# Exponentials over 1536 columns with two rings of three banks, in place of 1024 columns with three rings of two

## The chip, the cores and the metric

The kernel runs on one core of a Trainium2 chip. The metric is the device time of one execution in microseconds (us), a median over several runs; lower is better.

## What is computed

One transformer layer over 2048 tokens of 256 features: attention with 16 heads of 16 features, a residual and a layer norm, a gated feed-forward part with int8 weights, a residual and a layer norm. The change touches the attention alone, which is, cut to what matters:

```python
q, k, v = (X @ Wq + bq, X @ Wk + bk, X @ Wv + bv)      # (1, 2048, 256), split into 16 heads of 16
scores = einsum('bhqd,bhkd->bhqk', q, k) / sqrt(16)    # 16 heads x 2048 x 2048
attn = softmax(scores, axis=-1)
out = einsum('bhqk,bhkd->bhqd', attn, v)
x = layernorm(x + out @ Wo + bo)
```

## The kernel before

The program has three stages on one core: the projections to q, k and v (to about 48 us), the attention (about 53 to 564 us) and the output projection with the feed-forward part (to the end). Only the attention is touched.

**Units.** For each of the 16 heads the 2048 keys are cut into 16 tiles of 128 (`TT` = 16). One head with one key tile is called a unit here; there are 256. In a unit, TensorE makes the scores of 128 keys against all 2048 queries: four matmuls of 512 columns (`CH` = 4, `CW` = 512), each filling one bank of PSUM (line 1087). ScalarE takes exponentials of them, PSUM to SBUF, into `probs` (line 510). TensorE then multiplies the exponentials with v and a column of ones (`prob_times_v`, line 1061): four float32 matmuls, which the trace shows as two passes each, eight in all, and which add up in bank `ACC` = 6. This product runs two units behind the scores. So the order of TensorE, written out by hand, is: the four scores of unit u, then the product of unit u-2, then the four scores of unit u+1, and so on. There is no scheduler; each engine runs its own program in order and waits on semaphores.

**The banks before.** Banks 0 to 5 hold scores, as three rings of two. One exponential reads two banks (1024 columns), so a unit has two, its halves. Before the first score of a half, TensorE waits until the exponential three back has left those two banks; the semaphore `exp_done` counts exponentials:

```python
ring = (2 * n + half) % 3
pe.wait_ge(exp_done, 2 * u + half - 2)     # ahead of each pair of scores
pe.wait_ge(exp_done, 2 * (u - 1))          # ahead of the product of unit u-2
```

**The other side.** ScalarE waits with `scores_ready` for the two scores of its half, and ahead of the first half of a unit also with `pv_done` for the product of unit u-3, since `probs` holds three units. Heads 1 to 15 run in a hardware loop of five trips with three heads each; head 0 stands ahead of it.

**At a head's end** VectorE copies the finished accumulator out of bank 6 (line 730, `attn<-ps`), and TensorE waits for this copy (`attn_saved`) before the first product of the next head, which stands behind the scores of that head's third unit. SyncE refills the q and k of a head's slot once `scores_ready` has reached the end of the head that used it (`refill`).

Of the kernel before, what the change touches and what calls it, by code (L numbers as in the profile page):

```python
# [6 lines left out]
def layer_program(nc, X, Wq, bq, Wk, bk, Wv, bv, Wo, bo, w_gate, w_up, w_down, s_gate, s_up, s_down, out):  # L23
# [3 lines left out]
    ACT = mybir.ActivationFunctionType  # L27
# [3 lines left out]
    P = 128  # L31
    S, HID = X.shape[1], X.shape[2]
    NH = 16
# [3 lines left out]
    TT = S // P  # L37
    CW = 512
    CH = S // CW
# [8 lines left out]
    ROWS = MROW + 3  # L48
    LAG = 3
    VW = 32  # L50
    NSLOT = 3
    SCALE = float(HD) ** -0.5
    SAFE = 40.0
# [2 lines left out]
    with ExitStack() as ctx:  # L56
# [3 lines left out]
        def place(name, shape, dt, at=None):  # L60

            size = int(np.prod(shape[1:])) * {f32: 4, f32r: 4, i32: 4, bf16: 2, i8: 1}[dt]
            where = place_at[0] if at is None else at
            if at is None:
                place_at[0] += (size + 63) // 64 * 64
            return nc.alloc_sbuf_tensor_at(name, shape, dt, offset=where)
# [40 lines left out]
        minus_half = place("minus_half", [P, TPC], f32)  # L107
        q_stack = [place(f"q_stack{i}", [ROWS, S], bf16) for i in range(NSLOT)]
        k_stack = [place(f"k_stack{i}", [ROWS, S], bf16) for i in range(NSLOT)]
        v_slot = [place(f"v_slot{i}", [P, TT, VW], f32) for i in range(NSLOT)]  # L110

# [29 lines left out]
        probs = place("probs", [P, 3, CH, CW], f32, at)  # L141
# [2 lines left out]

        ps = ctx.enter_context(nc.psum_tensor("ps", [P, 8, CW], f32))
        ACC = 6

        def sem(name):
            return ctx.enter_context(nc.semaphore(name))
# [43 lines left out]
        bound_zero = sem("bound_zero")  # L193
        stack_loaded = [sem(f"stack_loaded{i}") for i in range(NSLOT)]
        v_slot_ready = sem("v_slot_ready")
        scores_ready = sem("scores_ready")
        exp_done = sem("exp_done")
        pv_done = sem("pv_done")
        attn_saved = sem("attn_saved")
# [50 lines left out]
        V_BANK = [4, 5, 4, 5, 4, 5, 4, 2]  # L250
# [3 lines left out]
        def _(sp):  # L254
# [9 lines left out]
            half = TPC // 2  # L264
# [36 lines left out]
            def load_stack(h, slot, done):  # L301

                for product in range(len(PRODUCTS)):
                    load_q(h, slot, product, done)
                    load_k(h, slot, product, done)
# [6 lines left out]

            def refill(h, slot):

                sp.wait_ge(scores_ready, (h - NSLOT + 1) * 2 * TT)
                load_stack(h, slot, stack_loaded[slot])
                load_shift(h, slot, stack_loaded[slot])


            sp.wait_ge(shift_zero, 2)  # L320
            for s in range(NSLOT):

# [37 lines left out]
            for h in range(NSLOT, NH):  # L360
                refill(h, h % NSLOT)
# [80 lines left out]
                nc.gpsimd.tensor_tensor(rstd[:, 2 * b:2 * b + 2], var_eps[:, 2 * b:2 * b + 2],  # L442
                                        minus_half[:, 0:2], ALU.pow).then_inc(ln2_rstd, 1)

        def three_heads(engine, head):

            head(0, 0)
            with engine.Fori(0, (NH - 1) // 3) as i:
                for j in range(1, 4):
                    head(i * 3 + j, j)  # L450

        @block.scalar
        def _(act):
            act.dma_start(w_raw[:, 0, :].rearrange("p (k n) -> p k n", k=KO),
# [26 lines left out]
            for n, (c, k) in enumerate(QK):  # L481
                parts, b_c = (q_parts, bq_c) if k < 2 else (k_parts, bk_c)
                if n == 0:
# [3 lines left out]
                                     bias=b_c[:, k % 2:k % 2 + 1]).then_inc(part1_ready, 1)  # L487
                nc.scalar.activation(squares[:, k, c * CW:(c + 1) * CW], ps[:, n % QK_BANKS, :], ACT.Square,
                                     bias=b_c[:, k % 2:k % 2 + 1]).then_inc(squares_ready, 1)
# [7 lines left out]
                                       ps[:, V_BANK[p], :].rearrange("p (a b) -> p a b", a=2)).then_inc(v_ready, 1)  # L497


            def head(h, j):  # L500
                for kt in range(TT):
                    u = h * TT + kt
                    for half in range(2):
                        ring = (2 * (j * TT + kt) + half) % 3

                        act.wait_ge(scores_ready, 2 * u + half + 1)
                        if half == 0 and not (j == 0 and kt < 3):

                            act.wait_ge(pv_done, u - 2)
                        nc.scalar.activation(  # L510
                            probs[:, (j * TT + kt) % 3, 2 * half:2 * half + 2, :].rearrange("p a b -> p (a b)"),
                            ps[:, 2 * ring:2 * ring + 2, :].rearrange("p a b -> p (a b)"),
                            ACT.Exp, bias=0.0, scale=SCALE).then_inc(exp_done, 1)


            act.wait_ge(xt_ready, 2 * CH)
            three_heads(act, head)

            act.wait_ge(warm_ready, 2)
            nc.scalar.activation(warm[:], minus_half[:], ACT.Silu)  # L520
# [48 lines left out]
            for b in range(2):  # L569
                i = 2 * b  # L570
                act.wait_ge(tail_mean, b + 1)
                nc.scalar.activation(out_tmp[:, i, :], r_tmp[:, i, :], ACT.Identity, scale=rstd[:, i:i + 1],
                                     bias=neg_mean[:, i:i + 1]).then_inc(tail_scaled, 1)

        @block.vector
        def _(dve):
# [350 lines left out]
        def _(pe):  # L927
# [57 lines left out]
            for n, (c, k) in enumerate(QK):  # L985
# [8 lines left out]
                if n >= QK_BANKS:  # L994
# [3 lines left out]
                i, m = k // 2, k % 2  # L998
# [3 lines left out]
                         first=(n == 0)).then_inc(proj_psum, 1)  # L1002
# [30 lines left out]
            with pe.If(need_exact > 0):  # L1033

                with pe.Fori(0, NH) as h:
                    pe.wait_ge(gen_loaded, (h + 1) * STACK)
                    for t in range(TT):
# [6 lines left out]
                        for b in range(CH):  # L1044
                            last = nc.tensor.matmul(ps[:, 4 * (t % 2) + b, :], q_stack[0][0:SROW, t * P:(t + 1) * P],
                                                    k_stack[0][0:SROW, b * CW:(b + 1) * CW], start=True, stop=True)
# [11 lines left out]
            def prob_times_v(slot, n, kt):  # L1058

                for q in range(CH):  # L1060
                    last = nc.tensor.matmul(ps[32 * q:32 * q + VW, ACC, :], v_slot[slot][:, kt, :],  # L1061
                                            probs[:, n % 3, q, :], start=(kt == 0), stop=(kt == TT - 1))
                last.then_inc(pv_done, 1)

            def head(h, j, i):
                slot, first = j % 3, (j == 0)
                for kt in range(TT):
                    u = h * TT + kt
                    n = j * TT + kt
                    if kt == 0:  # L1070

                        pe.wait_ge(stack_loaded[slot], (i + 1 + j // 3) * (STACK + SHIFT))

                        pe.wait_ge(bound_ready, 1 if first else 2 + slot)
                    if first and kt == 2:
                        pe.wait_ge(bound_ready, 2)
                    for half in range(2):
                        ring = (2 * n + half) % 3
                        if first and kt == 0 and half == 1:

                            pe.wait_ge(rest_ready, len(QK))
                            pe.wait_ge(v_ready, TT // 2)

                        if not (first and 2 * kt + half < 3):
                            pe.wait_ge(exp_done, 2 * u + half - 2)
                        for q in (2 * half, 2 * half + 1):
                            last = nc.tensor.matmul(ps[:, 2 * ring + q % 2, :],  # L1087
                                                    k_stack[slot][0:ROWS, kt * P:(kt + 1) * P],
                                                    q_stack[slot][0:ROWS, q * CW:(q + 1) * CW], start=True, stop=True)
                        last.then_inc(scores_ready, 1)  # L1090

                    if kt >= 2:
                        if kt == 2:
                            pe.wait_ge(v_slot_ready, h + 1)
                            if not first:

                                pe.wait_ge(attn_saved, h)
                        pe.wait_ge(exp_done, 2 * (u - 1))
                        prob_times_v(slot, n - 2, kt - 2)
                    elif not first:  # L1100
                        pe.wait_ge(exp_done, 2 * (u - 1))
                        prob_times_v((j - 1) % 3, n - 2, TT - 2 + kt)


            pe.wait_ge(ones_ready, NSLOT - 1)
            pe.wait_ge(ones_pool, 1)
            pe.wait_ge(ones_loaded, 16 * NSLOT)
            head(0, 0, 0)
            with pe.Fori(0, (NH - 1) // 3) as i:
                for j in range(1, 4):  # L1110
                    head(i * 3 + j, j, i)
            for kt in (TT - 2, TT - 1):
                pe.wait_ge(exp_done, 2 * ((NH - 1) * TT + kt + 1))
                prob_times_v(0, 3 * TT + kt, kt)


# [1 line left out]
            for g in range(8):  # L1118
# [4 lines left out]
                for k in range(8):  # L1123
                    last = nc.tensor.transpose(
                        ps[:, 2 * ug + k // 4, (k % 4) * P:(k % 4 + 1) * P],
                        attn[:, 8 * ug + k, HPB * ko:HPB * (ko + 1), :].rearrange("p r h -> p (r h)"), ident[:])
# [22 lines left out]
            for c, half, ko in steps:  # L1149
# [86 lines left out]
```

## Time and profile before

| | |
|---|---|
| median of 3 runs | 695.58 us (695.06 to 698.11) |
| span of the profiled execution | 694.9 us |
| TensorE matmul busy | 668.3 us, 96% |
| ScalarE busy | 580.7 us, 84% |
| VectorE busy | 153.7 us, 22% |
| exponentials, line 510 | 512 of 1024 columns, 495.2 us busy |
| scores, line 1087 | 1024 matmuls, 267.6 us busy |
| product with v, line 1061 | 2048 matmul passes, 272.5 us busy |

The profile gives one execution by its span, from the first to the last instruction. What lies around the span isn't in it; the median of the runs is 0.7 us above the span. Busy times of TensorE are unions of modelled, overlapping records.

### The profile page before, as it was taken

Reading aid. Unit: us, or ns where it says so; the run is one execution under the profiler, and the core shown is the slowest. Engines: PE = TensorE matmul, PEld = TensorE weight load, DVE = VectorE, ACT = ScalarE, POOL = GpSimd, SP = SyncE. Lnnn points to the kernel's source line nnn. Section 1 sums busy time; section 2 is a strip of 40 time slices with the busy share of each in tenths; the row PEclk is TensorE's granted clock in tenths of the full one; section 3 lists DMA queues with packets and bytes.
Section 4 is the critical chain, followed back from the end, with each engine's and each line's share of the span. In section 5 each row is a group of like instructions: output and inputs, shape, how many; then the busy total and the mean of one; then the engine's idle time right before and its main releaser. Section 6 shows DMA issues by size and latency. Waiting matters only on the chain.

```text
span 694.9 us, 10890 instructions
## 1 busy us (share of the span) xinstructions
PE 668.3 (96%) x4002; PEld 259.4 (37%) x4002; DVE 153.7 (22%) x305; ACT 580.7 (84%) x657; POOL 38.1 (5%) x47
## 2 busy tenths in 40 slices
PE   8979999999999999999999999999999999999994
PEld 7852222222222222222222222222222257788884
DVE  6772000000000000000000000000000047756766
ACT  5748999999999999999999999999999943744442
POOL 3215000000000000000000000003000001000002
PEclk9998999999999999999999999999999999999998
DMA  8066132140404041321404040413000000000001
GB/s 233 19 71 69 13 35 31 17 46 3 46 0 46 0 46 12 34 29 17 45 1 46 0 46 0 46 12 34 0 0 0 0 0 1 1 0 32 0 30 60
DMA packets 15428, 19.50 MB, mean 28 GB/s; under 512 B 5912, under 2 KB 12336, under 8 KB 15408
## 3 DMA queue, kind: packets, MB, share of 16 engines
q1 hardware_dynamic: 14592, 18.97, 20.2%
q10 hardware_dynamic: 816, 0.26, 0.1%
q8 instruction: 12, 0.20, 0.1%
q14 instruction: 8, 0.07, 0.0%
HBM read 4.34 MB, written 2.10 MB: 9 GB/s over the span
## 4 chain that ended last, share of the span: by engine, by line
PE 89%; DVE 5%; issue 4%; ACT 1%; POOL 1%; DMA 1%; POOLq 0%; SPq 0%; DVEq 0%
PE ps L1061 37%; PE ps L1087 36%; PE ps L1184 7%; PE ps L1167 4%; PE ps L966 4%; DMA x_tok<-in_L_attn_X 1%; DVE at L769 1%; DVE stats L785 1%; DVE h L870 1%; PE ps L950 1%; DVE r_tmp L831 1%; ACT sg L549 0%; POOL rstd L431 0%; DVE x_tok L778 0%; PE ps L1155 0%
## 5 line engine op out<-in xcount | busy, mean ns | idle before, releaser
L510 ACT ACTIVATE probs<-ps 128x1024 f32<-128x1024 f32 x512 | 495.2, 1021 | 19.8 <-PE ps L1087 12.5
L1061 PE MATMUL ps<-probs,v_slot 128*32 128x512 f32 x2048 | 272.5, 605 | 4.7 <-issue 4.7
L1087 PE MATMUL ps<-q_stack,k_stack 100*128 100x512 bf16 x1024 | 267.6, 385 | 5.6 <-DVE k_stack L675 5.6
L1087 PEld LDWEIGHTS ps<-q_stack,k_stack 100*128 100x128 bf16 x1024 | 79.7, 98 | 280.8 <-ACT probs L510 213.1
L730 DVE TENSOR_SCALAR attn<-ps 128x512 f32 (+1 forms) x16 | 16.4, 1028 | 488.5 <-PE ps L1061 488.5
L1061 PEld LDWEIGHTS ps<-probs,v_slot 128*32 128x32 f32 x2048 | 40.9, 108 | 114.6 <-ACT probs L510 94.7
L549 ACT ACTIVATE sg<-ps,sgate_c 128x512 f32<-128x512 f32 x32 | 22.1, 690 | 46.7 <-PE ps L1184 46.5
L1167 PE MATMUL ps<-wd,h_hi 128*128 128x256 f32 x128 | 32.2, 285 | 2.3 <-DVE r_tmp L831 2.1
L1167 PE MATMUL ps<-wd,h_lo 128*128 128x256 f32 x128 | 31.9, 283 | 0.0
L870 DVE SCALAR_TENSOR_TENSOR h<-ps,sup_c,sg 128x512 f32<-128x512 f32 x32 | 24.0, 750 | 27.0 <-ACT sg L549 26.2
L1167 PEld LDWEIGHTS ps<-wd,h_hi 128*128 128x128 f32 x128 | 24.3, 190 | 4.9 <-DVE r_tmp L831 3.4
L526 ACT ACTIVATE x_tok<-x_tok,neg_mean,rstd 128x256 f32<-128x256 f32 x16 | 8.3, 591 | 21.3 <-DVE neg_mean L799 21.3
L1184 PE MATMUL ps<-yt_hi,wg 128*128 (+1 forms) x64 | 25.5, 399 | 0.5 <-DVE h L870 0.3
L1184 PE MATMUL ps<-yt_lo,wg 128*128 (+1 forms) x64 | 25.3, 396 | 0.0
L1184 PE MATMUL ps<-yt_hi,wu 128*128 (+1 forms) x64 | 25.0, 391 | 0.0
L1184 PE MATMUL ps<-yt_lo,wu 128*128 (+1 forms) x64 | 24.9, 389 | 0.0
L1167 PEld LDWEIGHTS ps<-wd,h_lo 128*128 128x128 f32 x128 | 24.4, 191 | 0.9
L423 POOL CAST wg<-gate 128x2048 fp32r<-128x2048 int8 x1 | 1.9, 1891 | 409.3 <-DMA q_stack<-shift 409.3
L878 DVE TENSOR_TENSOR h_lo<-h,h_hi 128x512 fp32r<-128x512 f32 x32 | 21.8, 682 | 0.4
L558 ACT CAST h_hi<-h 128x512 fp32r<-128x512 f32 x32 | 19.6, 614 | 1.2 <-DVE h L870 1.2
L1155 PE MATMUL ps<-wo,at 128*128 128x256 f32 x64 | 14.6, 383 | 0.9 <-DVE at L769 0.8
L1184 PEld LDWEIGHTS ps<-yt_hi,wg 128*128 128x128 f32 x64 | 12.1, 190 | 2.5 <-DVE h L870 1.1
(100 smaller groups left out, 354.4 us busy)
## 6 DMA issues: line engine op xcount, KB each, us to landing
q_stack<-q_parts SPq DMA_DIRECT2D x16, 192.0 KB
k_stack<-k_parts SPq DMA_DIRECT2D x16, 192.0 KB
q_stack<-q_parts SPq DMA_DIRECT2D x16, 128.0 KB
k_stack<-k_parts SPq DMA_DIRECT2D x16, 128.0 KB
x_tok<-in_L_attn_X SPq DMA_DIRECT2D x3, 512.0 KB, 8.5
out<-out_tmp SPq DMA_DIRECT2D x3, 512.0 KB, 2.9
k_stack<-k_parts SPq DMA_DIRECT2D x16, 64.0 KB
q_stack<-q_parts SPq DMA_DIRECT2D x16, 64.0 KB
```

The costliest lines, as they stand in the source:

```text
L510: nc.scalar.activation(probs[:, (j * TT + kt) % 3, 2 * half:2 * half + 2, :].rearrange("p a b -> p (a b)"), ps[:, 2 * ring:2 * ring + 2, : ...
L549: nc.scalar.activation(sg[:, m % 2, :], ps[:, m % 2, :], ACT.Silu, scale=sgate_c[:, m:m + 1]).then_inc(silu_done, 1)
L558: nc.scalar.copy(h_hi[:, m - 1, :], h32[:, (m - 1) % 2, :]).then_inc(h_hi_ready, 1)
L730: nc.vector.tensor_scalar(attn[:, :, :, bass.ds(h, 1)], ps[:, ACC, :].rearrange("p (u r o) -> p u r o", r=NH, o=1), 1.0, None, ALU.mult).t ...
L870: nc.vector.scalar_tensor_tensor(h32[:, m % 2, :], ps[:, 2 + m % 2, :], sup_c[:, m:m + 1], sg[:, m % 2, :], ALU.mult, ALU.mult).then_inc(g ...
L878: nc.vector.tensor_tensor(h_lo[:, m - 1, :], h32[:, (m - 1) % 2, :], h_hi[:, m - 1, :].bitcast(f32), ALU.subtract).then_inc(h_ready, 1)
L966: last = nc.tensor.matmul(dst, w(ko), x(ko), start=(n == 0), stop=(n == len(terms) - 1))
L1061: last = nc.tensor.matmul(ps[32 * q:32 * q + VW, ACC, :], v_slot[slot][:, kt, :], probs[:, n % 3, q, :], start=(kt == 0), stop=(kt == TT - 1))
L1087: last = nc.tensor.matmul(ps[:, 2 * ring + q % 2, :], k_stack[slot][0:ROWS, kt * P:(kt + 1) * P], q_stack[slot][0:ROWS, q * CW:(q + 1) * C ...
L1155: last = nc.tensor.matmul(ps[:, b, half * HID:(half + 1) * HID], at32[:, ko, 2 * b + half, :, :].rearrange("p j u -> p (j u)"), wo[:, ko, ...
L1167: last = nc.tensor.matmul(ps[:, 4 + i, 0:HID], h[:, m, i * P:(i + 1) * P], wd[:, m, :], start=(m == 0 and j == 0), stop=(m == MT - 1 and j ...
L1184: last = nc.tensor.matmul(ps[:, bank, :], w[:, ko, m * P:(m + 1) * P], y[:, ko, bass.ds(c * CW, CW)], start=(ko == 0 and j == 0), stop=(ko ...
```

## The change

One exponential now reads three banks (`GROUP` = 3, 1536 columns), and banks 0 to 5 are two rings of three. Scores are counted bank by bank through the whole attention, b = 4n + q; bank b belongs to group b // 3, and group g uses the ring g % 2. Groups no longer end where units end: twelve banks are three units and four groups. There are 341 exponentials of three banks and a last one of one bank. `probs` is used as one ring of twelve banks. Every score matmul now signals `scores_ready`, where every second one did. TensorE waits ahead of each group's first score until the group two back is done. The order of the matmuls is unchanged: four scores, then the product of two units back.

```diff
+    GROUP = 3
+    UNIT = CH
...
+        probs_flat = probs[:].rearrange("p a b n -> p (a b) n")
+        def group_of(bank):
+            return bank // GROUP
...
-                sp.wait_ge(scores_ready, (h - NSLOT + 1) * 2 * TT)
+                sp.wait_ge(scores_ready, (h - NSLOT + 1) * TT * UNIT)
...
+            def exp_group(g, trips, banks, held):
+                first, ring = GROUP * g, 3 * UNIT
+                act.wait_ge(scores_ready, trips * GROUP + first + banks)
+                if held:
+                    act.wait_ge(pv_done, trips * GROUP // UNIT + (first + banks - 1 - ring) // UNIT + 1)
+                nc.scalar.activation(
+                    probs_flat[:, first % ring:first % ring + banks, :].rearrange("p a b -> p (a b)"),
+                    ps[:, GROUP * (g % 2):GROUP * (g % 2) + banks, :].rearrange("p a b -> p (a b)"),
+                    ACT.Exp, bias=0.0, scale=SCALE).then_inc(exp_done, 1)
...
+            for g in range(HEAD0):
+                exp_group(g, 0, GROUP, g >= 4)
+            with act.Fori(0, (NH - 1) // 3) as i:
+                for g in range(HEAD0, HEAD0 + TRIP):
+                    exp_group(g, i * TRIP, GROUP, True)
+            exp_group(HEAD0 + TRIP, ((NH - 1) // 3 - 1) * TRIP, 1, True)
...
-                        if not (first and 2 * kt + half < 3):
-                            pe.wait_ge(exp_done, 2 * u + half - 2)
-                        for q in (2 * half, 2 * half + 1):
-                            last = nc.tensor.matmul(ps[:, 2 * ring + q % 2, :],
+                    for q in range(UNIT):
+                        b = n * UNIT + q
+                        g = group_of(b)
+                        if b % GROUP == 0 and b >= 2 * GROUP:
+                            pe.wait_ge(exp_done, trips + g - 1)
+                        last = nc.tensor.matmul(ps[:, GROUP * (g % 2) + b % GROUP, :],
...
-                        pe.wait_ge(exp_done, 2 * (u - 1))
+                        pe.wait_ge(exp_done, trips + group_of((n - 2) * UNIT + UNIT - 1) + 1)
```

TensorE, head 0, three units. `ps<-q_stack,k_stack` is a score, `ps<-probs,v_slot` the product. Before:

```order
218 L1087 MATMUL ps<-q_stack_82,k_stack_85 128x512 [waits exp_done]
219 L1087 MATMUL ps<-q_stack_82,k_stack_85 128x512
220 L1087 MATMUL ps<-q_stack_82,k_stack_85 128x512 [waits exp_done]
221 L1087 MATMUL ps<-q_stack_82,k_stack_85 128x512
222 L1061 MATMUL ps<-probs,v_slot_88 32x512 [waits exp_done]
223 L1061 MATMUL ps<-probs,v_slot_88 32x512 x3
```

Every unit is the same there: two pairs of scores with a wait ahead of each, then the product. TensorE, the same place, now:

```order
226 L1076 MATMUL ps<-q_stack_82,k_stack_85 128x512 [waits exp_done]
227 L1076 MATMUL ps<-q_stack_82,k_stack_85 128x512 x2
228 L1076 MATMUL ps<-q_stack_82,k_stack_85 128x512 [waits exp_done]
229 L1049 MATMUL ps<-probs,v_slot_88 32x512 [waits exp_done]
230 L1049 MATMUL ps<-probs,v_slot_88 32x512 x3
231 L1076 MATMUL ps<-q_stack_82,k_stack_85 128x512 x2
232 L1076 MATMUL ps<-q_stack_82,k_stack_85 128x512 [waits exp_done]
233 L1076 MATMUL ps<-q_stack_82,k_stack_85 128x512
234 L1049 MATMUL ps<-probs,v_slot_88 32x512 [waits exp_done]
235 L1049 MATMUL ps<-probs,v_slot_88 32x512 x3
236 L1076 MATMUL ps<-q_stack_82,k_stack_85 128x512
237 L1076 MATMUL ps<-q_stack_82,k_stack_85 128x512 [waits exp_done]
```

The wait stands ahead of every third score, so its place moves through the units: in the first of three units ahead of the first and the fourth score, in the second ahead of the third, in the third ahead of the second. A product now lies inside two of every four groups.

ScalarE, the start of head 0, before:

```order
L510 ACTIVATE probs<-ps 128x1024 [waits scores_ready,xt_ready]
L510 ACTIVATE probs<-ps 128x1024 [waits scores_ready] x5
L510 ACTIVATE probs<-ps 128x1024 [waits pv_done,scores_ready]
L510 ACTIVATE probs<-ps 128x1024 [waits scores_ready]
```

and now:

```order
L491 ACTIVATE probs<-ps 128x1536 [waits scores_ready,xt_ready]
L491 ACTIVATE probs<-ps 128x1536 [waits scores_ready] x3
L491 ACTIVATE probs<-ps 128x1536 [waits pv_done,scores_ready] x17
```

Four exponentials cover what six did, and each of them behind the fourth waits for `pv_done` too.

## Rows read from the trace of the kernel before

**Rows 1.** The page, its parts on busy time and on granted clock.
```profile
PE 668.3 (96%) x4002; PEld 259.4 (37%) x4002; DVE 153.7 (22%) x305; ACT 580.7 (84%) x657; POOL 38.1 (5%) x47
...
PEclk9998999999999999999999999999999999999998
```

**Rows 2.** The page, costliest groups: busy us, mean ns of one, idle before.
```profile
L510 ACT ACTIVATE probs<-ps 128x1024 f32<-128x1024 f32 x512 | 495.2, 1021 | 19.8 <-PE ps L1087 12.5
L1061 PE MATMUL ps<-probs,v_slot 128*32 128x512 f32 x2048 | 272.5, 605 | 4.7 <-issue 4.7
L1087 PE MATMUL ps<-q_stack,k_stack 100*128 100x512 bf16 x1024 | 267.6, 385 | 5.6 <-DVE k_stack L675 5.6
```

**Rows 3.** Timeline inside the attention: start us, length us, instructions merged.
```profile
299.69 1.04 PE L1087 MATMUL ps<-q_stack,k_stack 100*128 100x512 bf16 x4
...
300.65 1.06 PE L1061 MATMUL ps<-probs,v_slot 128*32 128x512 f32 x8
...
301.65 1.04 PE L1087 MATMUL ps<-q_stack,k_stack 100*128 100x512 bf16 x4
...
309.52 1.04 PE L1087 MATMUL ps<-q_stack,k_stack 100*128 100x512 bf16 x4
```

**Rows 4.** Timelines of ScalarE and TensorE in short windows of that stretch.
```profile
299.29 2.07 ACT L510 ACTIVATE probs<-ps 128x1024 f32<-128x1024 f32 x2
...
300.33 1.94 ACT L510 ACTIVATE probs<-ps 128x1024 f32<-128x1024 f32 x2
...
299.69 0.60 PE L1087 MATMUL ps<-q_stack,k_stack 100*128 100x512 bf16 x2
```

**Rows 5.** ScalarE groups by form, of the whole program.
```profile
L496 ACT COPY v_all<-ps 128x512 f32<-128x512 f32 x8 | 4.7, 588 | 5.5 <-PE ps L966 5.5
...
L462 ACT ACTIVATE warm<-minus_half 128x4 f32<-128x4 f32 x1 | 0.2, 205 | 0.0
```

**Rows 6.** Timeline at the end of the attention.
```profile
561.78 1.02 ACT L510 ACTIVATE probs<-ps 128x1024 f32<-128x1024 f32 x1
...
562.85 0.13 PEld L1061 LDWEIGHTS ps<-probs,v_slot 128*32 128x32 f32 x4 [0.65 <-ACT probs L510]
...
562.49 1.04 PE L1061 MATMUL ps<-probs,v_slot 128*32 128x512 f32 x8
```

**Rows 7.** Timeline where one head ends and the next begins.
```profile
310.48 1.07 PE L1061 MATMUL ps<-probs,v_slot 128*32 128x512 f32 x8
...
311.48 1.04 PE L1087 MATMUL ps<-q_stack,k_stack 100*128 100x512 bf16 x4
311.74 1.03 DVE L730 TENSOR_SCALAR attn<-ps 128x512 f32 x1 [30.59 <-PE ps L1061]
...
312.87 1.07 PE L1061 MATMUL ps<-probs,v_slot 128*32 128x512 f32 x8 [0.35 <-issue]
```

**Rows 8.** Timeline at the start of the attention.
```profile
52.76 5.28 PE L1087 MATMUL ps<-q_stack,k_stack 100*128 100x512 bf16 x12 [5.55 <-DVE k_stack L675]
...
53.86 5.61 ACT L510 ACTIVATE probs<-ps 128x1024 f32<-128x1024 f32 x6 [6.03 <-PE ps L1087]
```

**Rows 9.** Stretches: length, busy us by engine, granted clock, DMA share, GB/s.
```profile
300.00:400.00 100.00, 98.99 (x604) 23.53 (x602) 3.84 (x6) 97.24 (x102) 0.00 (x0) 1.00 0.23 24
...
44.00:52.00 8.00, 3.20 (x28) 2.94 (x24) 4.23 (x11) 1.39 (x3) 0.37 (x1) 0.97 0.97 108
52.00:58.00 6.00, 5.25 (x16) 1.52 (x18) 4.62 (x9) 4.14 (x5) 0.90 (x1) 0.50 0.84 98
566.00:582.00 16.00, 15.09 (x95) 12.85 (x94) 12.60 (x28) 0.00 (x0) 0.30 (x1) 1.00 0.01 2
```

More of the change, by code:

```diff
@@ L443, in _ @@
                                         minus_half[:, 0:2], ALU.pow).then_inc(ln2_rstd, 1)
[L445 to L450, printed above, removed]
         @block.scalar
@@ L497, in _ @@
                                        ps[:, V_BANK[p], :].rearrange("p (a b) -> p a b", a=2)).then_inc(v_ready, 1)
[L500 to L513, printed above, removed]
-            act.wait_ge(xt_ready, 2 * CH)
-            three_heads(act, head)
+            def exp_group(g, trips, banks, held):
[7 more added lines that the diff above has]
+                    ACT.Exp, bias=0.0, scale=SCALE).then_inc(exp_done, 1)
+            HEAD0 = TT * UNIT // GROUP
+            TRIP = 3 * TT * UNIT // GROUP
+            act.wait_ge(xt_ready, 2 * CH)
+            for g in range(HEAD0):
[4 more added lines that the diff above has]
+            exp_group(HEAD0 + TRIP, ((NH - 1) // 3 - 1) * TRIP, 1, True)
             act.wait_ge(warm_ready, 2)
@@ L1063, in prob_times_v, with head @@
                 last.then_inc(pv_done, 1)
-            def head(h, j, i):
+            def head(j, i):
                 slot, first = j % 3, (j == 0)
+                trips = i * 3 * TT * UNIT // GROUP
                 for kt in range(TT):
-                    u = h * TT + kt
                     n = j * TT + kt
@@ L1076, in head @@
                         pe.wait_ge(bound_ready, 2)
-                    for half in range(2):
-                        ring = (2 * n + half) % 3
-                        if first and kt == 0 and half == 1:
+                    for q in range(UNIT):
+                        b = n * UNIT + q
+                        g = group_of(b)
+                        if first and b == V_BANK[-1]:
                             pe.wait_ge(rest_ready, len(QK))
                             pe.wait_ge(v_ready, TT // 2)
-                        if not (first and 2 * kt + half < 3):
-                            pe.wait_ge(exp_done, 2 * u + half - 2)
-                        for q in (2 * half, 2 * half + 1):
-                            last = nc.tensor.matmul(ps[:, 2 * ring + q % 2, :],
-                                                    k_stack[slot][0:ROWS, kt * P:(kt + 1) * P],
-                                                    q_stack[slot][0:ROWS, q * CW:(q + 1) * CW], start=True, stop=True)
+                        if b % GROUP == 0 and b >= 2 * GROUP:
+                            pe.wait_ge(exp_done, trips + g - 1)
+                        last = nc.tensor.matmul(ps[:, GROUP * (g % 2) + b % GROUP, :],
+                                                k_stack[slot][0:ROWS, kt * P:(kt + 1) * P],
+                                                q_stack[slot][0:ROWS, q * CW:(q + 1) * CW], start=True, stop=True)
                         last.then_inc(scores_ready, 1)
@@ L1093, in head @@
                         if kt == 2:
-                            pe.wait_ge(v_slot_ready, h + 1)
+                            pe.wait_ge(v_slot_ready, i * 3 + j + 1)
                             if not first:
-                                pe.wait_ge(attn_saved, h)
-                        pe.wait_ge(exp_done, 2 * (u - 1))
+                                pe.wait_ge(attn_saved, i * 3 + j)
+                        pe.wait_ge(exp_done, trips + group_of((n - 2) * UNIT + UNIT - 1) + 1)
                         prob_times_v(slot, n - 2, kt - 2)
                     elif not first:
-                        pe.wait_ge(exp_done, 2 * (u - 1))
+                        pe.wait_ge(exp_done, trips + group_of((n - 2) * UNIT + UNIT - 1) + 1)
                         prob_times_v((j - 1) % 3, n - 2, TT - 2 + kt)
@@ L1107, in _ @@
             pe.wait_ge(ones_loaded, 16 * NSLOT)
-            head(0, 0, 0)
+            head(0, 0)
             with pe.Fori(0, (NH - 1) // 3) as i:
                 for j in range(1, 4):
-                    head(i * 3 + j, j, i)
+                    head(j, i)
             for kt in (TT - 2, TT - 1):
-                pe.wait_ge(exp_done, 2 * ((NH - 1) * TT + kt + 1))
+                pe.wait_ge(exp_done, group_of(((NH - 1) * TT + kt + 1) * UNIT - 1) + 1)
                 prob_times_v(0, 3 * TT + kt, kt)
```

## The prediction

> **What bounds the kernel now.** I read the page first. TensorE is busy 96% of the span and ScalarE 84%, and the granted clock is at its upper level, 2.4 GHz, nearly throughout [rows 1]. Three lines carry the attention: the exponentials with 495 us on ScalarE, the scores and the products with 268 and 273 us on TensorE [rows 2]. In a stretch of 100 us both engines look full, 99.0 and 97.2 us busy [rows 9]. So busy time doesn't say which of the two sets the pace, and the timeline must.
>
> In the timeline the units follow each other evenly: scores at 299.69, product at 300.65, scores at 301.65, and five units from 299.69 to 309.52, so 1.966 us a unit [rows 3]. Does TensorE wait for an exponential there? Exponentials start at 299.29, 300.33 and 301.25 (299.29 + 2.07 - 1.02, and 300.33 + 1.94 - 1.02); their distances are 1.04 and 0.92 us in turn [rows 4]. The first two scores of the unit at 299.69 end at 300.29 and the next exponential starts at 300.33, 0.04 us behind them [rows 4]: ScalarE waits for TensorE once a unit. Call that exponential 2u. The scores at 299.69 need only exponential 2u-3, which began some 2 us earlier, at about 297.3, and ended at about 298.3. The second pair needs 2u-2, which began at 298.37 and ended at 299.39; that pair begins at 299.69 + 2 x 0.22 = 300.13, with 0.74 us to spare. (0.22 is the distance of two scores: 0.60 less the 0.38 that one lasts.) **TensorE waits for nothing and sets the pace; ScalarE has about 0.12 us of slack in a unit.** At a head's end TensorE does wait, for VectorE's copy: the product starts at 312.87, where 311.48 + 0.96 = 312.44 would be its turn, so 0.43 us [rows 7].
>
> **The change, part by part.**
>
> *The exponentials.* From 512 columns (0.588 us) to 1024 (1.02 us) one ScalarE instruction grows by 0.43 us [rows 2, 5], so I put 1536 columns at 1.02 + 0.43 = 1.45 us. From the 4-column activation, 0.205 us [rows 5], to 1024 columns it would be 0.41 a bank, hence 1.43; in proportion to columns 1.53. Back to back, behind one that was held up, the distance grows from 0.92 to 1.35 us (in proportion, 1.38). Per three units ScalarE needs 4 x 1.35 = 5.40 us in place of 6 x 0.92 = 5.52. TensorE takes 3 x 1.966 = 5.90, so what ScalarE saves is worth nothing by itself. The Trainium skill (ScalarE: Activation LUTs, What ACT_TABLE_LOAD costs) gives such an ACTIVATE 186 ns + 0.833 ns per column and an overlap of 93 ns: 1.04 us for 1024 columns, where the trace has 1.02, and 1.47 for 1536. By these figures the loop below would be 0.04 us longer.
>
> *The ring of two.* This is the term that decides. Number the scores of three units 0 to 11, the groups G0 (0 to 2), G1 (3 to 5), G2 (6 to 8), G3 (9 to 11). A group may start when the exponential two groups back is done. The order of TensorE is 0 1 2 3 product 4 5 6 7 product 8 9 10 11 product. Score 3, which opens G1, comes right behind 0, 1, 2, while it needs the exponential of the G3 before it. That one waits in turn behind the exponential of the G2 before, which needed score 8. So there is a closed loop, once every three units:
> - from the start of score 3 to the start of score 8: two units less the three distances from the first to the fourth score, 2 x 1.966 - 0.66 = 3.27 us (0.66 is 1.04 - 0.38) [rows 3];
> - score 8 until its record ends, 0.38, and 0.04 to the start of the exponential of G2 [rows 2, 4];
> - start of that of G2 to start of that of G3, back to back: 1.35;
> - the exponential of G3 until it is done: 1.45;
> - release of TensorE. At the end of the attention the last exponential ends at 561.78 + 1.02 = 562.80 and the weight load that waited for it starts at 562.85 [rows 6]. I take 0.06. At most it is 0.12: the product in question began by 562.92 (562.49 + 0.43).
>
> The sum is 3.27 + 0.38 + 0.04 + 1.35 + 1.45 + 0.06 = **6.55 us per three units against 5.90 now**: 0.65 more, 0.217 a unit. ScalarE then runs G2, G3 and G0 back to back and idles in front of G1 and G2, and TensorE stalls some 0.65 us ahead of score 3. The waits at scores 0, 6 and 9 cost little: with the same figures they come due within 0.1 us of TensorE's own time. Nothing else waits on that queue ahead of score 3; the product behind it waits too, and with it scores 4 and 5. Of the attention, 254 units lie behind the first two: 254 x 0.217 = +55.0 us.
>
> *The head ends.* The stall of 0.43 us now falls on a loop that has slack elsewhere. In a product behind score 3 the copy ends during the new stall; in one behind score 11 the delay is taken up by the next stall; in one behind score 7 it stays. A head has 16 units, one more than a multiple of three, so the place moves on and each case has 5 of 15 head ends: -10 x 0.43 = -4.3 us.
>
> *Start and end.* At the start twelve scores run without a pause at 0.43 us apart, at 1.2 GHz [rows 8, 9]. Now the first exponential starts one score later and the seventh score waits for it, but the first product only comes about 0.3 us later. At the end a one-bank exponential stands behind the last full one; that is within the loop's figures. +0.3 us. The pv_done waits on ScalarE cost nothing: the product asked for always stands ahead of the last score of the group, in TensorE's order. Twice as many signals by scores cost nothing either: in rows 4 the second score, which signals, is followed at the same distance. The refills of q and k wait for the same point of the program and have three heads' time.
>
> The sum: 55.0 - 4.3 + 0.3 = +51 us. On the span of 694.9 that is 745.9; the median of the runs is 0.7 above the span, and I carry that over: **746.5 us**.
>
> **The bounds of this case.** With 0.12 for the release, +5 us. With an exponential in proportion to its columns (+0.08 in its length, +0.03 in the distance), 0.11 x 85 = +9. With the flatter slope, -3. If head ends hide all or nothing, -2 or +4. Hence 738 to 757.
>
> **The rivals.**
>
> *ScalarE sets the pace (faster).* The mechanism lies in the fixed part of an exponential at line 510. The mean distance is 0.98 us, of which 2 x 0.43 are columns; 171 exponentials less at 0.12 each give -21 us, **675 us**; with the back-to-back distance of 0.92 it is -10 us. It decides if TensorE was held by exponentials, and if the loop above is shorter than 5.40 us. The Trainium skill (Perfetto Trace Analysis, Optimizing Scalar/DVE Operations) supports it: it gives ScalarE an overhead of some 51 ns an instruction on PSUM and says that grouping into larger operations can improve throughput if the engine is saturated. Its condition isn't met here: once a unit an exponential starts 0.04 us behind its scores [rows 4]. Chance 0.03.
>
> *No difference.* The ring's wait is hidden, by an early release or because I misplace it. The loop would have to lose 0.65 us, more than all its hand-overs together. 696 us, chance 0.03.
>
> *A smaller stall.* Around each product TensorE loses 0.09 us (0.31 from the last score to the product, where 0.22 would do; as much again behind it). Were all of this compressible when TensorE is late, 5 scores at 0.22 and four half products at 0.43 make 2.8 in place of 3.27; the loop is 6.08, which is +0.18 x 85 - 4 = +11 us: 707 us. Against it: the gaps are there in a unit in which nothing is awaited. Chance 0.05.
>
> *The clock falls.* TensorE will idle about a tenth of the attention. Before the attention it stood still for over 5 us and 52 to 58 ran at 0.50 [rows 8, 9], with scores 0.43 us apart. In 566 to 582, with waits of up to a microsecond and 15.1 of 16 us busy, it stayed at 1.00 [rows 9]. If a tenth of the attention ran at 1.2 GHz, some 8 loops would each be 5 x 0.21 + 4 x 0.43 = 2.8 us longer: +23, **770 us**. Chance 0.05.
>
> **How the numbers follow.** The forecast has 0.84. A measurement of this kernel can tell about 0.5% from no change. Faster 0.03 (the first rival), same 0.03, slower 0.94 (forecast, smaller stall, clock). The range 738 to 757 is the forecast's own, since the rivals hold less than 2 in 10 together.
>
> **What would show it.** Right: distances of exponentials in turn of about 1.35, 1.35, 2.1 and 1.7 us; 6.55 us from one third unit to the next; ahead of the fourth score of every third unit a gap of some 0.65 us that an exponential ends; exponentials busy for about 341 x 1.45 less 170 overlaps of 0.1, 477 us, in place of 495, while ScalarE's idle time before them rises to some 80; 1.45 us for one exponential; clock 1.00 all along. Wrong: even units of 1.97 us with the new groups (the ring doesn't bind), exponentials back to back throughout (ScalarE sets the pace), or score distances of 0.43 (the clock).

## The result, and the profile after

| | before | after |
|---|---|---|
| median of 4 runs | 695.64 us | 755.32 us (755.13 to 756.81) |
| ratio | | 1.0859 (95% interval 1.0838 to 1.0879) |
| span of the profiled execution | 694.9 us | 752.9 us |
| TensorE / ScalarE busy | 96% / 84% | 91% / 75% |

The changed kernel is 59.7 us slower, 8.6%. It was forecast at 746.5 us, in a range of 738 to 757. Of the experiments below, one run (1080.14 us, at a mean granted clock of 0.557, one of four of the kernel with the order over 16 scores and scores_ready first) was in a slower state: it is in that kernel's median and not in its ratio.

The page of the changed kernel, granted clock, the chain that ended last, and the costliest groups (busy us, mean ns of one, idle before and what ended it), which answer to [rows 1, 2]:

```profile
PEclk9989999999999999999999999999999999999999
...
PE 57%; issue 18%; ACT 18%; DVE 5%; ACTq 1%; POOL 1%; DMA 1%; POOLq 0%; SPq 0%; DVEq 0%
...
L491 ACT ACTIVATE probs<-ps 128x1536 f32<-128x1536 f32 x342 | 477.3, 1449 | 97.3 <-PE ps L1076 97.3
L1076 PE MATMUL ps<-q_stack,k_stack 100*128 100x512 bf16 x1024 | 286.7, 387 | 47.4 <-ACT probs L491 42.0
L1049 PE MATMUL ps<-probs,v_slot 128*32 128x512 f32 x2048 | 273.2, 606 | 2.9 <-issue 2.9
```

Each engine now waits for the other. ScalarE's exponentials became cheaper in sum (477.3 us against 495.2), but it stood idle for 97.3 us ahead of them, where it was 19.8. TensorE, which waited for no exponential in the even part of the attention, stood idle for 42.0 us ahead of scores, ended by exponentials; since its records are modelled and overlap, the true stall is longer than this (from the first score to the last product the attention took 570.4 us, where it was 510.6). The chain of waits, 89% TensorE before, now runs through ScalarE for 18%. The clock stayed at its upper level through the even part of the attention.

The timeline of the changed kernel, TensorE and ScalarE, in windows inside a head (start us, length us, what, count). Score 3 of three units starts at 312.50, score 8 at 315.79, the next score 3 at 319.14:

```profile
312.50 0.39 PE L1076 MATMUL ps<-q_stack,k_stack 100*128 100x512 bf16 x1 [0.52 <-ACT probs L491]
...
313.82 1.04 PE L1076 MATMUL ps<-q_stack,k_stack 100*128 100x512 bf16 x4
314.79 1.07 PE L1049 MATMUL ps<-probs,v_slot 128*32 128x512 f32 x8
...
315.79 0.39 PE L1076 MATMUL ps<-q_stack,k_stack 100*128 100x512 bf16 x1
...
316.29 2.79 ACT L491 ACTIVATE probs<-ps 128x1536 f32<-128x1536 f32 x2 [0.30 <-PE ps L1076]
...
317.64 2.79 ACT L491 ACTIVATE probs<-ps 128x1536 f32<-128x1536 f32 x2
...
319.14 0.39 PE L1076 MATMUL ps<-q_stack,k_stack 100*128 100x512 bf16 x1 [0.52 <-ACT probs L491]
```

This is the loop of the forecast, link by link: from score 3 to score 8 3.29 us (forecast 3.27); score 8 until 316.18 and then **0.11** to the exponential (forecast 0.38 + 0.04); 1.35 from the exponential of G2 to that of G3 (1.35); that one ends at 319.08, as 316.29 + 2.79 says, 1.44 long (1.45); score 3 again 0.06 later (0.06). The sum is 6.64 us per three units, where TensorE alone took 5.90.

### The profile page after: what moved, and what is told of

It reads as the page before. It is cut to its first block, busy times and chain, and to the rows that moved or that the text cites. A ratio compares the mean times of both kernels' runs of the same rounds, so it can differ in the third digit from the quotient of the medians.

```text
span 752.9 us, 10479 instructions
## 1 busy us (share of the span) xinstructions
PE 686.1 (91%) x4002; PEld 256.9 (34%) x4002; DVE 153.6 (20%) x305; ACT 562.2 (75%) x487; POOL 38.1 (5%) x47
## 4 chain that ended last, share of the span: by engine, by line
PE 57%; issue 18%; ACT 18%; DVE 5%; ACTq 1%; POOL 1%; DMA 1%; POOLq 0%; SPq 0%; DVEq 0%
PE ps L1049 23%; PE ps L1076 20%; ACT probs L491 17%; PE ps L1172 6%; PE ps L1155 4%; PE ps L954 3%; DMA x_tok<-in_L_attn_X 1%; ACTq L490 1%; DVE at L757 1%; DVE stats L773 1%; DVE h L858 1%; DVE r_tmp L819 0%; ACT sg L537 0%; POOL rstd L422 0%; PE ps L938 0%
## 5 line engine op out<-in xcount | busy, mean ns | idle before, releaser
L491 ACT ACTIVATE probs<-ps 128x1536 f32<-128x1536 f32 x342 | 477.3, 1449 | 97.3 <-PE ps L1076 97.3
L1076 PE MATMUL ps<-q_stack,k_stack 100*128 100x512 bf16 x1024 | 286.7, 387 | 47.4 <-ACT probs L491 42.0
```

The lines of the kernel that those rows point to most:

```text
L491: nc.scalar.activation(probs_flat[:, first % ring:first % ring + banks, :].rearrange("p a b -> p (a b)"), ps[:, GROUP * (g % 2):GROUP * (g ...
L1076: last = nc.tensor.matmul(ps[:, GROUP * (g % 2) + b % GROUP, :], k_stack[slot][0:ROWS, kt * P:(kt + 1) * P], q_stack[slot][0:ROWS, q * CW: ...
```

## The experiments

All were built from the changed kernel, with its constants for the rings made free (banks per exponential, number of rings) and, where said, TensorE's order given by a table.

### Is the ring of two the cause, or the form of the code?

Groups of two banks in three rings, as before the change, in the changed program:

```diff
-    GROUP = 3
+    GROUP = 2
+    RINGS = 3
...
-                            pe.wait_ge(exp_done, trips + g - 1)
+                            pe.wait_ge(exp_done, trips + g - RINGS + 1)
-                        last = nc.tensor.matmul(ps[:, GROUP * (g % 2) + b % GROUP, :],
+                        last = nc.tensor.matmul(ps[:, GROUP * (g % RINGS) + b % GROUP, :],
```

Expected:

> The changed program with groups of two banks and three rings, as before the change, but with its own counting (a signal from every score, pv_done ahead of every exponential, the register instruction between the waits). Theory (the ring of two decides): TensorE waits for nothing and the time is that of the kernel before, 695.6 us within 0.3%. Rival (the form of the code costs: twice the signals, more waits and register instructions): some of the 60 us stay, a time over 700.

Measured: 695.95 us, ratio to the kernel before 1.0001 (0.9987 to 1.0014). The doubled signals, the additional waits for pv_done and the register work cost nothing that can be measured, as long as TensorE waits for nothing.

Then the same with `RINGS = 2`, so rings of two without larger exponentials.

> The changed program with groups of two banks and only two rings (banks 4 and 5 idle), so exponentials of 1024 columns. Theory (rings of two close a loop through TensorE's products): a stall ahead of the scores that follow a product's neighbour, +33 to +35 us on the kernel before with the hand-over at 0.115: 730 us (724 to 736). Rival A (three-bank exponentials are what costs): the time of the kernel before, 695.6. Rival B (every ring of two costs the same): 755.

Measured: 733.82 us, ratio 1.0535 (1.0518 to 1.0553). Taking a ring away costs 37.5 us with exponentials of the old size. ScalarE in that kernel, exponentials in fours:

```profile
300.29 3.90 ACT L493 ACTIVATE probs<-ps 128x1024 f32<-128x1024 f32 x4 [0.39 <-PE ps L1077]
304.53 3.90 ACT L493 ACTIVATE probs<-ps 128x1024 f32<-128x1024 f32 x4 [0.34 <-PE ps L1077]
```

Two units take 4.24 us instead of 3.93: 0.15 a unit, 254 times, 39 us. So most of the loss comes with taking away the third ring. This kernel also leaves two banks idle, but banks alone aren't the cause: the changed kernel fills all six in two rings and is 21.5 us slower still. I put that rest down to the exponential that must end as a whole (1.45 us, not 1.02) before its banks come free; no run separates this.

### Is it the place of the products?

The same exponentials, groups and rings as in the changed kernel, but TensorE's products stand behind the 3rd, 6th and 12th of twelve scores instead of the 4th, 8th and 12th:

```diff
+            PERIOD, BEHIND, BACK = 12, (3, 6, 12), 2
+            def products_behind(b):
+                return [(b - b % PERIOD) // UNIT + k - BACK for k, at in enumerate(BEHIND) if at == b % PERIOD + 1]
...
                         last.then_inc(scores_ready, 1)
+                        for m in products_behind(b):
+                            product(m, j, i, trips)
```

> The changed kernel with the same exponentials, groups and rings, but TensorE's order moved to the groups: of twelve scores, the products stand behind the 3rd, the 6th and the 12th instead of the 4th, 8th and 12th. Theory (the loop from score 3 over two products to score 8 is what costs): the scores of G1 now come behind a product and have no product inside, no loop is longer than TensorE's own 5.90 us; 695.6 + 1 to 5: 699 us (696 to 702). Rival (exponentials of three banks, the signals or the clock cost by themselves): still near 755.

Measured: 701.82 us, ratio 1.0089 (1.007 to 1.0108). Moving two of three products by one or two scores takes back 53.5 of the 59.7 us. TensorE's rows there:

```profile
300.20 0.82 PE L1097 MATMUL ps<-q_stack,k_stack 100*128 100x512 bf16 x3
300.95 1.06 PE L1051 MATMUL ps<-probs,v_slot 128*32 128x512 f32 x8
301.95 0.82 PE L1097 MATMUL ps<-q_stack,k_stack 100*128 100x512 bf16 x3
302.70 1.06 PE L1051 MATMUL ps<-probs,v_slot 128*32 128x512 f32 x8
303.70 1.51 PE L1097 MATMUL ps<-q_stack,k_stack 100*128 100x512 bf16 x6
305.14 1.07 PE L1051 MATMUL ps<-probs,v_slot 128*32 128x512 f32 x8
306.14 0.60 PE L1097 MATMUL ps<-q_stack,k_stack 100*128 100x512 bf16 x2
```

From 300.20 to 306.14 it is 5.94 us for three units, near the 5.90 of before. A product now stands ahead of the first score of G1 and none lies inside a group, so each exponential gets its three banks in one run.

### Where did the missing 9 us go?

The order in which ScalarE waits, turned round:

```diff
-                act.wait_ge(scores_ready, trips * GROUP + first + banks)
                 if held:
                     act.wait_ge(pv_done, trips * GROUP // UNIT + (first + banks - 1 - ring) // UNIT + 1)
+                act.wait_ge(scores_ready, trips * GROUP + first + banks)
```

> The changed kernel with one thing altered: ScalarE waits for pv_done first and for scores_ready second, so that the register instruction which prepares the first wait no longer stands between the scores' signal and the exponential. Theory (hand-over): in the loop trips an exponential starts 0.115 us behind its last score's record instead of 0.037; the closed loop is 6.636 us per three units, and without the 0.078 it is 6.56, so 85 x 0.078 = 6.6 us less than the changed kernel: 748.7 us (747 to 750). Rival: the 9 us missing in the forecast come from something else (longer exponentials, more signals, release of TensorE); then 755.3, no difference.

Measured: 750.67 us, ratio to the kernel before 1.0785 (1.0767 to 1.0803), so 4.65 us less than the changed kernel: a miss of the band (747 to 750) by 0.7 us, but clear of the rival's zero. In the even part the step is the expected one. The copies of the accumulator, one a head, stand three heads apart, first in the changed kernel:

```profile
234.04 1.02 DVE L718 TENSOR_SCALAR attn<-ps 128x512 f32 x1 [34.54 <-PE ps L1049]
...
340.62 1.02 DVE L718 TENSOR_SCALAR attn<-ps 128x512 f32 x1 [34.53 <-PE ps L1049]
```

then with the waits turned round:

```profile
234.05 1.03 DVE L720 TENSOR_SCALAR attn<-ps 128x512 f32 x1 [34.15 <-PE ps L1051]
...
339.38 1.03 DVE L720 TENSOR_SCALAR attn<-ps 128x512 f32 x1 [34.15 <-PE ps L1051]
```

That is 106.58 and 105.33 us for 16 loops, so 0.078 us less in each, and 6.2 for the 80 loops of heads 1 to 15. The expectation counted 85, but the five of head 0 had no register instruction to save: there the turned waits took 6.617 us a loop where it had been 6.557, and the head 0.4 us more. Another 1.4 us were lost ahead of the attention, whose first score came at 52.3 us and not at 50.9; over the profiled executions here it comes at 50.9 to 52.8.

Why the hand-over differs can be read in ScalarE's order inside the hardware loop. Of the kernel before, six of the 48 first halves of a trip look like the first pair of these rows, the others like the last:

```
L509 REGISTER_ALU [waits scores_ready]
L510 ACTIVATE probs<-ps 128x1024 [waits pv_done]
...
L510 ACTIVATE probs<-ps 128x1024 [waits pv_done,scores_ready]
```

In the changed kernel 48 of the 64 exponentials of a trip have the first form: a register instruction waits for the scores and the exponential is issued behind it. The traces agree in number. Before, 30 exponentials that started late, so with ScalarE idle ahead of them (six in each of five trips), came 0.12 or 0.13 us behind the record of their last score and 208 came 0.04 behind it; after, 163 came 0.12 to 0.16 and 10, all in head 0, came 0.04 behind; with the waits turned round 164 came 0.04 and 9, again all in head 0, came 0.10 behind. So in head 0, which is written out, the turn made the hand-over longer: there an instruction of its own waits for the scores after the turn, and for pv_done before it.

The same turn in the order over twelve scores:

> The order over twelve scores (products behind the 3rd, 6th and 12th) with groups of three in two rings, and pv_done waited for ahead of scores_ready, so a hand-over of 0.037 in place of 0.115 us. Theory: the loop there is near TensorE's own 5.90 us; each loop loses up to 0.078 less, so 2 to 3 us less than the same order without it (701.8): 698 to 700 us. Rival (TensorE alone sets that time): 701.8, no difference.

Measured: 698.01 us, ratio 1.0019 (1.001 to 1.0028), 3.8 us less than without it. So exponentials of three banks in two rings can run at the old pace, within 0.2%, once the order of TensorE and of the waits fits them. They aren't faster, since TensorE sets the pace: three units take 5.897 us there and 5.898 in the kernel before.

### Can TensorE's own order be made shorter?

I took it that every change between scores and a product costs TensorE about 0.09 us [rows 3, 4]; at a head's end 0.43 us are lost [rows 7]. With groups of two in three rings, pv_done first, and `PERIOD, BEHIND, BACK = 16, (6, 6, 12, 16), 2`:

> A version meant to beat both. Groups of two banks in three rings as before the change, pv_done waited for ahead of scores_ready, and TensorE's order over 16 scores with four products: two products in a row behind the 6th score, one behind the 12th, one behind the 16th. Theory (TensorE's own order sets the pace, and each change between scores and a product costs it some 0.09 us): per four units one pair of changes less, 0.18 us, and at a head's end more work lies between the last product and the first one of the next head, so less of the 0.43 us stall. ScalarE needs 8 x 0.904 to 0.921 = 7.2 to 7.4 us per four units against TensorE's 7.68. 64 x 0.18 = 12 us and up to 6 at the head ends, less what the rings give back: 680 to 686 us. Rival (the rings close a new loop at the longer run without products): 696 or more.

Measured: **685.57 us, ratio 0.9844 (0.9831 to 0.9858)**, 1.6% faster than the kernel before, which is little but clear of the noise. Its rows:

```profile
300.79 1.63 PE L1096 MATMUL ps<-q_stack,k_stack 100*128 100x512 bf16 x6
302.35 1.92 PE L1050 MATMUL ps<-probs,v_slot 128*32 128x512 f32 x16
304.21 1.47 PE L1096 MATMUL ps<-q_stack,k_stack 100*128 100x512 bf16 x6
305.61 1.06 PE L1050 MATMUL ps<-probs,v_slot 128*32 128x512 f32 x8
306.60 1.04 PE L1096 MATMUL ps<-q_stack,k_stack 100*128 100x512 bf16 x4
307.57 1.06 PE L1050 MATMUL ps<-probs,v_slot 128*32 128x512 f32 x8
308.57 0.61 PE L1096 MATMUL ps<-q_stack,k_stack 100*128 100x512 bf16 x2
```

Four units take 308.57 - 300.79 = 7.78 us, where four of 1.966 are 7.86. By these rows a second product right behind the first adds 1.86 - 0.99 = 0.87 us, and four more scores in a run add 4 x 0.216 = 0.86, so 1.73 where a unit by itself takes 1.97. The order alone would then give about 7.62, less than the 7.68 expected, and 0.16 went to the rings again: the first run of six scores takes 1.56 us to its product and the second 1.40, and in the first a weight load waits for an exponential:

```profile
301.81 0.11 PEld L1096 LDWEIGHTS ps<-q_stack,k_stack 100*128 100x128 bf16 x2 [0.48 <-ACT probs L493]
```

The 11 us have two sources of one size. The even part gives 64 x 0.085 = 5.4 us. The heads follow each other every 31.12 us, four times 7.78, where it was 31.84 = 16 x 1.966 + 0.39; so nothing is lost at a head's end any more, which gives 15 x 0.39 = 5.9.

The same order with scores_ready waited for first:

> The order over 16 scores with four products, groups of two in three rings, but with scores_ready waited for ahead of pv_done, as in the kernel before and in the changed one. Theory: where ScalarE has little slack left, the hand-over of 0.115 in place of 0.037 us costs again, up to 0.078 for each of the 64 stretches of four units: 3 to 5 us more than with pv_done first (685.6): 689 to 691. Rival (the whole gain is the order's): 685.6, no difference.

Measured: 686.21 us, ratio 0.9856 (0.9836 to 0.9875); no difference, where 689 to 691 was expected. My theory fell here. The trace says why: of the exponentials that came late in this kernel all but one started 0.04 us behind their scores. Inside the loop it is one in eight, always at the same place of the order, and ahead of it no register instruction waits for the scores. So the gain is the order's (against the kernel with `RINGS = 3` and the old order, 695.95 us, this one differs in the order alone), and the hand-over costs only where it lies on the exponentials that are waited for.

One bank per exponential in six rings, with pv_done waited for first, to measure what an instruction costs. First in TensorE's old order:

> One bank per exponential, six rings of one, TensorE's order as before (four scores, one product). Theory: ScalarE's 4 x 0.478 to 0.495 = 1.91 to 1.98 us per unit against TensorE's 1.966; same as the kernel before, 696 us, if the fixed part of the distance is at most 0.065 us. Rival (a smaller exponential costs more): each 0.01 us more per exponential adds 10 us, so over 700 tells the fixed part.

Measured: 705.15 us, ratio 1.0113 (1.0097 to 1.0129). Then with eight scores and two products in turn, and room for four units in `probs`:

> One bank per exponential, six rings of one, probs for four units, TensorE with eight scores and then two products. Theory: TensorE alone would need 3.69 us per two units in place of 3.93. ScalarE needs 8 exponentials of 512 columns; if the fixed part of the back-to-back distance is 0.05 us, 8 x 0.478 = 3.82 and the time is 675 to 680; if it is 0.07, 3.96 and about 692. Rival (more instructions on ScalarE, with its register work, cost more than 0.07 each): over 700. It measures the fixed part of a back-to-back exponential.

Measured: 694.96 us, ratio 0.9971 (0.9961 to 0.998). The chains of waits of the two kernels, the single banks in TensorE's old order first:

```profile
PE 85%; DVE 5%; issue 5%; ACT 2%; POOL 1%; DMA 1%; ACTq 0%; POOLq 0%; DVEq 0%; SPq 0%
```

```profile
ACT 45%; PE 23%; issue 22%; DVE 5%; ACTq 3%; POOL 1%; DMA 1%; POOLq 0%; DVEq 0%
```

In both the commonest distance of two exponentials is 0.48 us, 0.05 above the 0.43 of the columns. By the two expectations that meant 696 us for the first and 675 to 680 for the second, so both missed, and the time doesn't tell the fixed part, as I had thought it would. The traces show what does.

In the second, rows of TensorE, its weight load and ScalarE over two units, each from a window of the timeline:

```profile
211.63 1.91 PE L1096 MATMUL ps<-q_stack,k_stack 100*128 100x512 bf16 x7
...
211.83 1.26 ACT L493 ACTIVATE probs<-ps 128x512 f32<-128x512 f32 x2
...
213.14 0.10 PEld L1096 LDWEIGHTS ps<-q_stack,k_stack 100*128 100x128 bf16 x1 [0.40 <-ACT probs L493]
...
213.47 1.92 PE L1050 MATMUL ps<-probs,v_slot 128*32 128x512 f32 x16
215.32 2.13 PE L1096 MATMUL ps<-q_stack,k_stack 100*128 100x512 bf16 x8
```

This is a ring's loop once more. The eighth score waits for the second exponential (211.83 + 1.26 = 213.09), starts 0.06 later, and both products follow it; the next first score comes at 215.32, its exponential 0.39 + 0.04 behind, at 215.75, 3.92 us after that of 211.83. Eight distances of 0.478 would be 3.82: ScalarE waits 0.1 us for scores in each loop, so it isn't saturated even here.

In the first the units follow each other every 1.966 us, as in the kernel before. Its 9 us are lost in four places, at the starts of heads 4, 7, 10 and 13, where the hardware loop turns: each costs 2.1 to 2.3 us more than the same place in the kernel before. Head 4:

```profile
180.70 1.07 PE L1050 MATMUL ps<-probs,v_slot 128*32 128x512 f32 x8
181.70 1.41 PE L1077 MATMUL ps<-q_stack,k_stack 100*128 100x512 bf16 x4
...
186.68 3.53 ACT L493 ACTIVATE probs<-ps 128x512 f32<-128x512 f32 x7 [2.06 <-PE ps L1050]
...
187.34 1.86 PE L1077 MATMUL ps<-q_stack,k_stack 100*128 100x512 bf16 x4 [0.93 <-ACT probs L493]
```

ScalarE stands still for 2.06 us until 186.68, although the scores of its exponential had ended by 183.11 and the product that frees its part of `probs` by 181.77, and TensorE then waits for it. The second kernel loses 5.4 us at the same places, the kernel before and the changed one nothing beyond a usual head end. What holds ScalarE there, in a trip with twice as many exponentials, is left open.

## Why the prediction was right, and where it was short

**What bounds.** Right. TensorE waited for no exponential before, and saved work on ScalarE was worth nothing: exponentials were busy for 477.3 us, as forecast (477), and the kernel got slower by 8.6%. The rival by which ScalarE sets the pace is out, and so is that of no difference.

**The exponential.** Right: 1.449 us against 1.45, and 1.35 between two. The commonest distances for one, two and three banks are 0.478, 0.90 to 0.92 and 1.33 to 1.35: 0.427 a bank, the slope of [rows 2, 5], and 0.05 to 0.07 fixed. Behind that stands the Trainium skill (Perfetto Trace Analysis, Optimizing Scalar/DVE Operations), which gives some 51 ns of overhead for ScalarE on PSUM; these runs agree. Its advice to group operations has a condition, a saturated engine, and no kernel here met it: in the kernel before ScalarE waited for scores once a unit, and even with single banks and pairs of products it waited 0.1 us in every two units. From two banks to three there was nothing to gain.

**The ring of two.** Right as a mechanism, with the stall ahead of score 3 where it was forecast. It was short by 0.085 us a loop, 6.635 against 6.55, which is 6.8 us over the 80 loops of heads 1 to 15. The term that was sized too small is "0.38, and 0.04 to the start of the exponential of G2": it measured 0.39 and 0.115. The 0.04 was read from an exponential of the kernel before whose wait had no register instruction behind it; after the change 48 of 64 have one, and the hand-over is 0.115. The turned waits gave 0.078 of the 0.085 back, and in head 0 of the changed kernel, where the hand-over was 0.037, the even loops took 6.557 us, the forecast's 6.55. I had looked at ScalarE's order in head 0, which runs outside the hardware loop and needs no registers, and not inside it.

**The smaller stall** was a rival with 0.05. Nothing of it was seen: TensorE's gaps around a product are the same in a late unit (319.14 to 319.46 there, 0.32 us, against 0.31 before).

**The head ends.** Right. Three heads take 106.58 us where 16 loops of 6.636 are 106.18, so one head end in three still costs 0.4 us. Over heads 1 to 15, with the end of the attention, 3.7 us came back of the 4.3.

**Start and clock.** Short by about 1.2 us: head 0 took 36.5 us, 4.5 more than before, where 14 units at 0.217 and the 0.3 are 3.3. In the windows of the start, the granted clock (third number from the end) of the kernel before stands in [rows 9]; of the changed one:

```profile
52.00:58.00 6.00, 5.68 (x18) 1.06 (x16) 2.77 (x6) 5.33 (x4) 2.66 (x3) 0.50 0.92 109
58.00:60.00 2.00, 2.00 (x8) 0.43 (x4) 0.00 (x0) 0.25 (x1) 2.00 (x2) 0.53 0.95 98
```

It stays at the lower level until 59.9 us, although the attention began 1.8 us earlier in that execution. Whether the stalls of the first scores keep it down is open. In the profiled executions of all kernels with two rings it was so. But it was also so in one of the two nearly equal kernels with the order over 16 scores, whose TensorE was busy all the time, first with pv_done waited for first, then with scores_ready first:

```profile
58.00:60.00 2.00, 2.00 (x14) 0.47 (x13) 0.00 (x0) 1.62 (x2) 2.00 (x3) 1.00 0.97 100
```

```profile
58.00:60.00 2.00, 2.00 (x12) 0.49 (x12) 0.00 (x0) 0.74 (x1) 2.00 (x3) 0.54 0.94 96
```

Their first heads took 31.7 and 33.0 us, so there the longer stay at the lower level went with 1.3 us, about what the forecast lacks in head 0.

The rival of a clock that falls in mid-attention is out: it stayed at 1.00 with TensorE busy 92.0 of 100 us.

**From span to time.** 1.7 us of the miss. I carried over 0.7 us between span and median, but they were of different executions. Where the profiled execution's own time is given, it lies 2.2 us above the span (755.13 against 752.9).

So of the 8.8 us above the forecast, 6.8 are the loop, 1.7 the step from span to time, 1.2 the first head and 0.6 the head ends. The shorter part ahead of the attention in this execution (50.9 against 52.8 us to the first score) takes 1.8 off again, and 0.3 stays unexplained. The mechanism was right. That the time still lay within the range was in part luck: the range was made for the release, the exponential's length and the head ends, and allowed nothing for the hand-over.

## What to carry to other kernels

Count the rings in time, not in banks: with two rings the release of one, the refill and the other's work form a closed loop, and whatever the producer does in between (here a product of 1 us) is in it. Add up that loop before making a transfer larger; if it is longer than the bound engine's own period, move the other work to the edges of the groups, which was worth 53 of 60 us here. And look at the order of an engine inside its hardware loop, not only in the part written out: a register instruction between the wait that comes due last and the work is paid at each hand-over that others wait for. Turning the waits moved it out of the way in the loop and made the hand-over longer in head 0, so the order has to be read for each.

## What the runs showed of the hardware that I had not expected

- A register instruction between the awaited signal and the ScalarE instruction costs 0.08 us at the hand-over (0.115 against 0.037 behind the record of the last matmul), and an instruction that only waits costs 0.06 there (0.098, in head 0 with the waits turned). Neither costs anything where nobody waits for ScalarE: with groups of two in three rings 229 hand-overs were of 0.12 us or more, and the time was that of the kernel before.
- ScalarE's distance from one exponential to the next is 0.427 us per 512 columns and 0.05 to 0.07 fixed, from one bank to three, across bank borders too.
- TensorE's weight load follows the end of the exponential it waits for by 0.051 us and the matmul starts 0.055 behind that end, in nearly every loop of the changed kernel.
- With single banks ScalarE stood still for 1.3 to 2.1 us twice at each of four turns of its hardware loop, with nothing left to wait for that the trace shows.
- The record of an exponential of 512 columns lasts 0.60 us behind an idle stretch and 0.77 to 0.84 in the kernel with eight scores and two products, where they follow 0.478 apart; the score that waits for one there starts 0.056 us behind the end of that longer record.
